# Attention: each query and value projection unit in a step of its own, and the weighted sum in two sweeps

## The reference, cut to what matters

```python
xn = layernorm(x)                        # x: 8 sequences x 2048 rows x 256
qkv = xn @ W_qkv                         # q, k, v of 256 columns each
scores = q @ k.T / 16                    # causal: keys after the query are masked
attn = softmax(scores)
out = x + attn @ v + ffn(xn)             # ffn: a shared expert and 32 routed ones, top 1
```

## Time and profile before

| | |
|---|---|
| median of 3 runs | 2519.98 us (2518.7 to 2520.93) |
| profiled execution, its own time | 2518.56 us |
| its span | 2516.5 us |
| TensorE busy over the span | 2414.3 us (96%) |
| VectorE, ScalarE, GpSimd busy | 1631.3, 1250.2, 1097.1 us |
| attention stage, about | 1445 to 2516 us |

### The profile page before, as it was taken

One profiled execution on the slowest core, in us unless ns is written; L12 is line 12 of the kernel. 1 busy time (PEld: TensorE's weight loads), 2 busy tenths in 40 slices (PEclk: granted clock), 3 DMA queues, 4 the chain that ended last, 5 costly groups with the idle time before them and its releaser, 6 DMA issues. The chain is left out here.

```text
span 2516.5 us, 51725 instructions
## 1 busy us (share of the span) xinstructions
PE 2414.3 (96%) x16569; PEld 2201.3 (87%) x16569; DVE 1631.3 (65%) x3665; ACT 1250.2 (50%) x2285; POOL 1097.1 (44%) x1115
## 2 busy tenths in 40 slices
PE   7999999999779999999999888999999999999997
PEld 5888888888679999999999767988888888888887
DVE  7777777775867777777777535464655555555554
ACT  3333333333545566556556434555555555555554
POOL 1111111110134444444444307666666666666667
PEclk9999999999889999999999999999999999999999
DMA  4434433442457777777777723232323233323321
GB/s 143 151 125 141 141 135 134 138 145 101 154 180 242 239 236 232 244 234 235 233 234 235 218 86 119 73 126 74 123 79 105 87 107 95 105 95 103 99 68 55
DMA packets 257028, 369.38 MB, mean 147 GB/s; under 512 B 18448, under 2 KB 187920, under 8 KB 256912
## 3 DMA queue, kind: packets, MB, share of 16 engines
q1 hardware_dynamic: 242896, 329.60, 38.9%
q0 software_dynamic: 14016, 38.29, 6.1%
HBM read 254.57 MB, written 113.25 MB: 146 GB/s over the span
## 5 line engine op out<-in xcount | busy, mean ns | idle before, releaser
L1145 POOL TENSOR_TENSOR t_p_lo<-t_score,t_p_hi 128x512 fp32r<-128x512 f32 (+1 forms) x320 | 359.9, 1135 | 276.8 <-ACT t_score L1265 205.1
L1257 ACT COPY t_score<-t_psS 128x512 f32<-128x512 f32 (+1 forms) x320 | 167.4, 523 | 335.4 <-PE t_psS L71 216.0
L1349 PE MATMUL t_psO<-t_v_hi,t_p_hi 128*128 128x258 f32 x1088 | 319.1, 293 | 14.7 <-POOL t_p_lo L1145 14.1
L1351 PE MATMUL t_psO<-t_v_hi,t_p_lo 128*128 128x258 f32 x1088 | 307.9, 283 | 0.0
L1353 PE MATMUL t_psO<-t_v_lo,t_p_hi 128*128 128x256 f32 x1088 | 306.9, 282 | 0.0
L832 DVE TENSOR_TENSOR e_wlo<-e_raw,e_whi 128x1024 fp32r<-128x1024 f32 x162 | 198.0, 1222 | 152.0 <-ACT e_whi L875 152.0
L808 POOL DMA_INDIRECT e_xg<-xs_rows,e_slot x164 | 248.2, 1513 | 97.0 <-POOL e_slot L804 63.3
L1191 DVE TENSOR_TENSOR t_top<-t_top,t_psS 128x512 f32<-128x512 f32 (+3 forms) x264 | 155.1, 587 | 152.1 <-ACT t_score L1257 150.2
L69 PE MATMUL t_psS<-t_q_hi,t_x_hi 128*128 128x512 f32 (+3 forms) x640 | 236.0, 369 | 6.3 <-DVE t_q_lo L1167 1.7
L70 PE MATMUL t_psS<-t_q_hi,t_x_lo 128*128 128x512 f32 (+3 forms) x640 | 233.3, 365 | 0.0
L71 PE MATMUL t_psS<-t_q_lo,t_x_hi 128*128 128x512 f32 (+3 forms) x640 | 233.1, 364 | 0.0
(11 more groups left out here) (199 smaller groups left out, 7728.8 us busy)
## 6 DMA issues: line engine op xcount, KB each, us to landing
e_raw<-in_L_ffn_routed_gate_w SPq DMA_DIRECT2D x83, 512.0 KB, 3.9
e_raw<-in_L_ffn_routed_up_w SPq DMA_DIRECT2D x83, 512.0 KB, 4.8
e_raw<-in_L_ffn_routed_down_w SPq DMA_DIRECT2D x82, 512.0 KB, 4.2
routed_rows<-e_dout SPq DMA_DIRECT2D x80, 256.0 KB, 3.5
a_xt<-in_L_attn_x SPq DMA_DIRECT2D x32, 512.0 KB, 4.5
xT_high<-a_xT_hi SPq DMA_DIRECT2D x32, 512.0 KB, 3.7
xT_low<-a_xT_lo SPq DMA_DIRECT2D x32, 512.0 KB, 3.9
xs_rows<-a_xs SPq DMA_DIRECT2D x32, 512.0 KB, 3.0
```

The costliest lines, as they stand in the source:

```text
L1145: g_.tensor_tensor(p_lo[:, t % LR, c0:], score[:, t % SR, c0:], p_hi[:, t % HR, c0:].bitcast(F32), ALU.subtract).then_inc(lo_ok, 1)
L1257: s.copy(score[:, t % SR, c0:], psS[:, n % BANKS, c0:]).then_inc(u_act, 1)
L1349: nc.tensor.matmul(psO[:, a, 0:W], p_hi[:, kp, cols], v_hi[:, kv, j % J], start=j == 0, stop=False, skip_group_check=True)
L1351: nc.tensor.matmul(psO[:, a, 0:W], p_lo[:, t % LR, cols], v_hi[:, kv, j % J], start=False, stop=False, skip_group_check=True)
```

## The change

The second query unit and the second value unit of each group move by a step or two, so that no step has two units of a kind: query units stand at places 37, 39, 1, 3, 9, 11, 21, 23 and value units at 10, 12, 14, 16, 22, 24, 34, 36. The first group of all keeps both query units in step 0. `weigh` waits for `exp_ok` (p_hi is there), makes the passes with p_hi for all blocks, then waits for `lo_ok` (p_lo is there) and makes the passes with p_lo. The number of matmuls, their shapes and all other engines' work stay the same.

```diff
--- before.py
+++ after.py
@@ -971,13 +971,11 @@
         self.first = [self.at[b, G, 0] for b in range(B) for G in range(GB)]
         self.last = [self.at[b, G, J * (G + 1) - 1] for b in range(B) for G in range(GB)]
         self.NGR = B * GB
-        q_step = {}
+        q_step, v_step = {}, {}
         for g in range(self.NGR):
-            q_step.setdefault(max(0, self.first[g] - 3), []).append(g)
-        v_step = {}
-        for g in range(self.NGR):
-            for u in range(J // 2):
-                v_step.setdefault(self.first[g] + 10 + u, []).append((g, u))
+            for u in range(2):
+                q_step.setdefault(max(0, self.first[g] - 3 + 2 * u), []).append((g, u))
+                v_step.setdefault(self.first[g] + 10 + 2 * u, []).append((g, u))
         self.q_step, self.v_step = q_step, v_step
         self.q_unit, self.v_unit, self.s_unit = {}, {}, []
         self.split, self.tops = [], []
@@ -991,11 +989,10 @@
             self.base_step.setdefault(t + self.LAG - self.LOW, []).append(r)
         n = 0
         for t in range(self.T):
-            for g in q_step.get(t, ()):
-                for c in range(2):
-                    self.q_unit[g, c] = n
-                    self.split.append(n)
-                    n += 1
+            for g, c in q_step.get(t, ()):
+                self.q_unit[g, c] = n
+                self.split.append(n)
+                n += 1
             for g, u in v_step.get(t, ()):
                 self.v_unit[g, u] = n
                 self.split.append(n)
@@ -1216,9 +1213,8 @@
                                        op0=ALU.mult, op1=ALU.add).then_inc(o_ok, 1)
 
             for step in range(T + LAG + 2):
-                for g in plan.q_step.get(step, ()):
-                    for c in range(C):
-                        q_low(g, c)
+                for g, c in plan.q_step.get(step, ()):
+                    q_low(g, c)
                 for g, u in plan.v_step.get(step, ()):
                     v_low(g, u)
                 if 0 <= step - LAG - 1 < T:
@@ -1265,9 +1261,8 @@
                 s.activation(p, p, ACT.Exp).then_inc(exp_ok, 1)
 
             for step in range(T + LAG + 2):
-                for g in plan.q_step.get(step, ()):
-                    for c in range(C):
-                        q_high(g, c)
+                for g, c in plan.q_step.get(step, ()):
+                    q_high(g, c)
                 for g, u in plan.v_step.get(step, ()):
                     v_high(g, u)
                 if step < T:
@@ -1340,24 +1335,25 @@
                 b, G, j = plan.tiles[t]
                 g, kv, kp = b * GB + G, (b * GB + j // J) % VR, t % HR
                 wait(pe, split_ok, plan.splits[plan.v_unit[b * GB + j // J, (j % J) // 2]])
-                wait(pe, lo_ok, t + 1)
+                wait(pe, exp_ok, t + 1)
                 for a in range(plan.cut(t), J):
                     cols = slice(a * P, (a + 1) * P)
-                    last = j == J * G + a
                     if j == 0:
                         wait(pe, o_ok, (g - 1) * J + a + 1)
                     nc.tensor.matmul(psO[:, a, 0:W], p_hi[:, kp, cols], v_hi[:, kv, j % J], start=j == 0, stop=False,
                                      skip_group_check=True)
-                    nc.tensor.matmul(psO[:, a, 0:W], p_lo[:, t % LR, cols], v_hi[:, kv, j % J], start=False, stop=False,
+                    nc.tensor.matmul(psO[:, a, 0:D], p_hi[:, kp, cols], v_lo[:, kv, j % J, 0:D], start=False, stop=False,
                                      skip_group_check=True)
-                    mm = nc.tensor.matmul(psO[:, a, 0:D], p_hi[:, kp, cols], v_lo[:, kv, j % J, 0:D], start=False, stop=last,
-                                          skip_group_check=True)
+                wait(pe, lo_ok, t + 1)
+                for a in range(plan.cut(t), J):
+                    cols = slice(a * P, (a + 1) * P)
+                    mm = nc.tensor.matmul(psO[:, a, 0:W], p_lo[:, t % LR, cols], v_hi[:, kv, j % J], start=False,
+                                          stop=j == J * G + a, skip_group_check=True)
                 mm.then_inc(pv_mm, 1)
 
             for step in range(T + LAG):
-                for g in plan.q_step.get(step, ()):
-                    for c in range(C):
-                        queries(g, c)
+                for g, c in plan.q_step.get(step, ()):
+                    queries(g, c)
                 for g, u in plan.v_step.get(step, ()):
                     values(g, u)
                 if step < T:
```

## The result

The changed kernel takes 2489.1 us (median of four runs, 2487.87 to 2489.7) against 2520.45 us; the ratio is 0.9875 with a 95% interval of 0.9859 to 0.9891. The forecast was 2489. The profiled execution spans 2487.5 us where it was 2516.5, so 29.0 us less.

What follows compares the result with a forecast made beforehand. TensorE is busy nearly throughout the attention stage, so only its gaps and low-clock stretches can be won. 25.6 + 5.5 - 5.0 + 2.7 + 2.4 = 31.2 us off, giving 2489 us, range 2481 to 2498 (0.70).

Steps and rivals of the forecast that it cites:

- The boundary: At seven sequence boundaries `spread` meets GpSimd later, so the wait for the copy and the half clock go: 25.6 us won.
- The hole in GpSimd's chain: At the boundary GpSimd idles from 1697.50 to 1698.3; `spread` falls into it and takes 0.7 to 1.0 us.
- 9.0 us for the clock: After six of seven boundary waits, the half-clock stretch goes, 1.5 us each.
- Query units apart: At other query steps scores no longer wait 0.26 us for a unit's low part; 21 places, 5.5 us won.
- the loss with `o_ok`: At places 37 and 9 the first `weigh` waits for `output` before block 3; 14 places, 5.0 us lost.
- The second unit's new readers: First scores of a group read the second unit one step on; nothing charged, bound 0.2 us for 28 places.
- The start: With one query unit in step 21, GpSimd's chain starts 1.4 us sooner and p_hi matmuls fill the wait: 2.7 us won.
- the 1.3 us of p_hi matmuls: At the start, six p_hi matmuls of one `weigh` run inside the p_lo wait, winning 1.3 us.
- The end: Moved value unit starts GpSimd's last chain 1.4 us sooner, p_hi matmuls fill the last wait, 1.0 us: 2.4 us won.
- The sum: All terms together take 31.2 us off the profiled execution: span 2516.5 becomes 2485.3, median 2489 us.
- same stationary operand twice: Rival, chance 0.04: in `weigh` one load serves two passes, shortening a slot; 6.5 us more won, 2482.
- the rival in which the boundary stays: Rival, chance 0.14: `spread` again meets two p_low end to end; only 5.6 us won, 2514.

Runs made afterwards that it cites:

- spread_psum: The kernel before, with the reduction writing its row maxima into PSUM so `spread` reads one operand from SBUF and one from PSUM; 2492.26 us, ratio 0.9883.
- q_at_38: The changed kernel with the second query unit one step earlier (places 38, 2, 10, 22); 2518.22 us, ratio 0.9996 against the kernel before.
- fill_wait: The kernel before, with 36 useless matmuls between the first and second query unit at each sequence boundary; 2511.47 us, ratio 0.9958.
- plan_only: The changed kernel with `weigh` in its old order, so only the units are moved; 2485.14 us, ratio 0.9859 against the kernel before.
- early_rows: The kernel before, with only the first row blocks' additions due up to 8 steps earlier; 2512.31 us, ratio 0.9963.
- v_old: The moved units with old `weigh`, but value units back at places 10, 11, 14, 15, 22, 23, 34, 35; 2487.74 us, ratio 0.9864 against the kernel before.
- sweeps_only: The kernel before with the new `weigh` alone, units where they stood; 2525.14 us, ratio 1.0014.
- copy_first: The kernel before with one swap on VectorE, `highest(step)` ahead of `row_max`; 2517.42 us, ratio 0.9986.

## Why the prediction was right, step by step

**The boundary** (25.6 us) was right, in mechanism and in size. One sequence took (2343.83 - 1565.39) / 6 = 129.7 us before and 125.7 after; the prediction had 3.9 less. With `spread_psum`, which changes nothing but `spread`, it takes 754.66 / 6 = 125.8, so 4.0 is what the boundary is worth; the forecast had 3.9, 2.36 of wait and 1.5 of half clock. The hole in GpSimd's chain was forecast from 0.2 us ahead of `spread` to 0.6 after it starts; it is 0.13 and 0.83. Its end was forecast from `exps` (1696.20 + 0.62, moved by 1.40); in the trace it is `weigh` that ends it, a little later, which the prediction had not looked at and which only helped. At step 40 there is nothing to spare on the first side, so the 0.2 us was a narrow margin. `q_at_38` shows that the hole is what counts, and `fill_wait` that 9.0 us for the clock was right (8.8).

**Query units apart and the loss with `o_ok`** (5.5 won, 5.0 lost) balanced, as forecast. `plan_only`, without the loss, has 750.03 us for six sequences, 28.4 less than before, of which 23.8 are the boundary (`spread_psum`); the 4.6 left are 0.77 a sequence, near three times 0.26. The places are not quite those of the forecast. The gap ahead of the scores is gone at places 9 and 21, but at place 37, which now stands right behind a step with a value unit, most of it is left, 0.20 us of 0.26:

```profile
1806.25 0.40 PE L71 MATMUL t_psS<-t_x_lo,keep_a_hi 128*128 128x512 f32 x1
...
1806.68 0.41 PE L69 MATMUL t_psS<-t_q_hi,t_x_hi 128*128 128x384 f32 x1
```

In exchange `spread_psum` has a gap of 0.26 us at place 1 too (1695.86 to 1696.35), which the moved unit takes away. The changed kernel gives back 754.09 - 750.03 = 4.1 over six. The timeline of TensorE in the changed kernel at step 89 (place 9), where blocks begin with L1343:

```profile
1717.54 0.37 PE L1343 MATMUL t_psO<-t_v_hi,t_p_hi 128*128 128x258 f32 x1
...
1718.11 0.28 PE L1343 MATMUL t_psO<-t_v_hi,t_p_hi 128*128 128x258 f32 x1
1718.23 0.28 PE L1345 MATMUL t_psO<-t_v_lo,t_p_hi 128*128 128x256 f32 x1
1718.62 0.39 PE L1343 MATMUL t_psO<-t_v_hi,t_p_hi 128*128 128x258 f32 x1
1718.85 0.28 PE L1345 MATMUL t_psO<-t_v_lo,t_p_hi 128*128 128x256 f32 x1
```

and VectorE's output ahead of it:

```profile
1718.08 0.49 DVE L1212 SCALAR_TENSOR_TENSOR t_outb<-t_psO,t_rinv,t_base 128x256 f32<-128x256 f32 x1
```

Blocks 1 and 2 start 0.24 apart; block 3 should start at 1718.35, and starts at 1718.62, when `output` (1718.08 + 0.49) is done. The first slot after it is 0.23, not 0.12, so such a wait costs 0.11 more than its length. The places were forecast only in part: by the lengths of the `weigh` blocks, 0.37 us go at place 9, 0.12 at place 37, where I had 0.36, and 0.25 at place 29, which I had left out as it has no unit. Together 0.74 us in each of seven sequences, 5.2: that the sum of 5.0 was met is in part luck.

**The second unit's new readers** wait for nothing: the scores at places 0, 4, 12 and 24 start without a gap in the six sequences.

**The start** (2.7 us) is the step that failed; 0.2 came. GpSimd's first p_low started at 1506.60 and not at 1505.5: counted from the stage's first matmul it came 0.6 us sooner and not 1.4. In the first 20 steps, where no `weigh` lies between them, the spaced units cost more: from the first matmul to the copy of step 20's scores they took 51.94 us where they took 51.09, and TensorE's waits for the low part of a query unit between 1455 and 1500 us went from 0.3 us (one) to 1.7 (three). And the 1.3 us of p_hi matmuls done inside the wait won about nothing: from GpSimd's second p_low to the `weigh` of tile 2, TensorE takes 5.2 us where it took 5.3. The changed kernel there:

```profile
1521.35 1.68 POOL L1142 TENSOR_TENSOR t_p_lo<-t_score,t_p_hi 128x384 fp32r<-128x384 f32 x2
1522.38 0.59 ACT L1253 COPY t_score<-t_psS 128x512 f32<-128x512 f32 x1 [7.38 <-POOL t_p_lo L1142]
...
1522.40 0.63 PE L1350 MATMUL t_psO<-t_v_hi,t_p_lo 128*128 128x258 f32 x3 [3.22 <-POOL t_p_lo L1142]
...
1523.00 0.69 DVE L1185 TENSOR_TENSOR t_top<-t_score,t_psS 128x512 f32<-128x512 f32 x1 [7.92 <-ACT t_score L1253]
...
1523.84 0.77 PE L69 MATMUL t_psS<-t_q_hi,t_x_hi 128*128 128x512 f32 x1 [0.81 <-DVE t_top L1185]
```

ScalarE's copy of the scores stands 7.38 us for the same p_low, which must free a slot of the score ring (`keep_score` waits for `lo_ok` of 24 tiles before), VectorE's `highest` for ScalarE, and TensorE, after only three p_lo matmuls, 0.81 us for VectorE. I looked at one wait behind this p_low, and there were two. The loss with `o_ok` at places 29 and 37, 0.4 us, falls into this stretch as well. `early_rows` shows what the place is worth, by taking the additions from between: 7.2 us up to step 40, 8.8 by the median.

**The end** (2.4 us) was right: 2.5 from step 319 on. The moved value unit gives 1.5 (`plan_only` 44.45 against 45.96 in `v_old`), the sweeps 1.0.

**The sum** was 31.2 us of span and came out as 29.0; of the start 2.5 us were missing, the rest gave 0.3 more than forecast. The median fell by 31.4, so that it met the forecast to 0.1 us is in part luck: I had put the median 1.4 above the profiled run, and this time it lay 0.6 below it.

**The rivals.** A slot of `weigh` did not get shorter by having the same stationary operand twice: a full tile's 12 matmuls after full scores take 1.435 us in the changed kernel and 1.434 in `plan_only` (medians). `q_at_38` is the rival in which the boundary stays, made on purpose: it was forecast at 2514 and took 2518. Of the 5.1 us that the forecast gave it for start and end, 0.7 and 2.5 came.

**Open:** five of 53 runs of the kernel before (two of 27, two of 11, one of 11, and none of the first four) took 2529.2 to 2529.7 us, some 9 us over their medians. That is the size of the one late `spread` seen in `v_old`, but no profile fell on such a run. The median of `sweeps_only` lies 4.8 us over that of before, when the spans of the profiled runs differ by 1.6: 1.2 is what the `o_ok` wait costs less what the end wins, and the profiled run has one clock fall (1.5 us) less than the profile of before. Whether the slower runs have more of them is not shown. Open is also why `spread`, once kept out, got in at a gap of 0.08 us between two additions at the boundary, but right behind a p_low, with no gap in the trace, in the 4.80 us of `copy_first`.

## What to carry to other kernels

Two engines that meet at a fixed offset in every period can lose, or win, the whole of a stall by 0.1 us: look in the timeline at what starts just ahead of the long instruction, and at what each of the two follows, and move work that lies between these two causes. A long instruction whose minimum is five times shorter is worth a question before any reordering; taking its operand from PSUM alone gave 28.0 us, where the change gave 31.4. When waits are moved rather than removed, count every reader of the late thing, not only the first, and let one half of an edit run without the other: here the second half cost 4 us.

## What the runs showed of the hardware

A VectorE product of two SBUF operands took 3.70 us instead of 0.69 while GpSimd ran two p_low and an addition end to end. It ended 0.5 us after a gap of 0.08 us between this addition and the next, and the next took 1.06 us instead of 0.74. In `copy_first` one took 4.80 us over three p_low and ended 0.6 us after them, with no gap in the trace, and the addition behind them took 1.21 us. With one operand in PSUM the product took 0.69 us every time. A wait of TensorE of 2.4 us was followed by some 3.4 us at half the clock at six of seven places in one execution, at none in `copy_first`, where the waits are 1.0 and 1.5 us, and at none when 36 useless matmuls of 128 columns filled 2.18 us of it, which made the kernel 8.8 us faster.
